# Feed-forward stage of a cross-attention block: sums of h and low parts moved from GpSimd to VectorE, squares moved to ScalarE, one set of weights kept over the change of batches, x1 + beta made beside x1

## The reference

```python
# attention block: 16 query heads, 4 key/value heads, head size 96, keys from 512 + 64 rows
x1 = x + attention(layernorm(x), ctx, Wq, Wk, Wv) @ Wo.T
# feed-forward block
z = layernorm(x1)
h = relu(z @ up_w) ** 2                       # 1024 -> 2048
r = sum(top_k(z @ gate_w, 2))                 # one factor per row
moe = ((z @ fc1_w) @ expert_w) * r            # 1024 -> 512 -> 512
y = h @ down_w + moe @ fc2_w                  # -> 1024
out = x1 + layernorm(y) * gamma + beta
```

## Time and profile before

| | us |
|---|---|
| median of 3 runs | 2124.26 (2122.04 to 2125.34) |
| the profiled execution | 2126.14 |
| its span | 2124.4 |
| PE busy | 1998.0 (94%) |
| DVE busy | 1251.8 (59%) |
| POOL busy | 1083.4 (51%) |
| ACT busy | 747.1 (35%) |
| output projection, tiles 0 to 15 | up to about 1216 |
| first product of the feed-forward | 1216 to 1692 |
| second product, norm and store | 1692 to 2124 |

### The profile page before, as it was taken

The page is one execution under the profiler, slowest core; times in us unless marked ns, Lnnn a source line. Parts: engine busy times, 40 slices in busy tenths (PEclk is TensorE's granted clock), DMA queues, the critical chain, the costliest instruction groups (busy, mean ns, idle before and its releaser), DMA issues.

```text
span 2124.4 us, 28447 instructions
## 1 busy us (share of the span) xinstructions
PE 1998.0 (94%) x9068; PEld 1656.9 (78%) x9068; DVE 1251.8 (59%) x1611; ACT 747.1 (35%) x1194; POOL 1083.4 (51%) x686
## 2 busy tenths in 40 slices
PE   8999999999999999999999779987799979999796
PEld 7888888888888888888887566866578768888685
DVE  4231312278888888812233479879778743456979
ACT  5021211167777777722110322123222233332131
POOL 2533030157777777652122156655765755456565
PEclk9999999999999999999999889988899989999998
DMA  6743433635566555345677665574343576765653
GB/s 198 263 152 138 168 119 100 174 96 147 151 157 157 149 147 146 102 150 180 188 250 229 232 178 198 195 231 169 119 149 139 176 243 198 242 198 170 218 184 136
DMA packets 352829, 368.32 MB, mean 173 GB/s; under 512 B 148704, under 2 KB 247008, under 8 KB 350304
## 3 DMA queue, kind: packets, MB, share of 16 engines
q1 hardware_dynamic: 284416, 303.56, 44.8%
q10 hardware_dynamic: 68320, 63.58, 11.0%
HBM read 241.99 MB, written 124.80 MB: 173 GB/s over the span
## 4 chain that ended last, share of the span: by engine, by line
PE 74%; DVE 10%; DMA 5%; issue 4%; POOL 3%; SPq 2%; ACT 1%; ACTq 1%; DVEq 0%; POOLq 0%
PE psum L139 22%; PE psum L140 22%; PE psum L141 22%; PE psum L1009 3%; POOL staging L2223 2%; DVE operands L1841 2%; DMA operands<-h_operand_scratch 2%; SPq L1355 1%; DMA operands<-o_scratch 1%; DMA z_turned_scratch<-plain 1%; ACTq L1355 1%; DVE plain L2523 1%; PE psum L1056 1%; PE psum L1036 1%; PE psum L1055 1%
## 5 line engine op out<-in xcount | busy, mean ns | idle before, releaser
L139 PE MATMUL psum<-operands 128*128 128x512 f32 (+3 forms) x2728 | 1062.2, 389 | 105.0 <-POOL operands L2370 24.4
L140 PE MATMUL psum<-operands 128*128 128x512 f32 (+3 forms) x2728 | 1058.3, 388 | 0.0
L141 PE MATMUL psum<-operands 128*128 128x512 f32 (+3 forms) x2728 | 1054.6, 387 | 0.0
L139 PEld LDWEIGHTS psum<-operands 128*128 128x128 f32 (+1 forms) x2728 | 519.3, 190 | 206.9 <-issue 34.9
L141 PEld LDWEIGHTS psum<-operands 128*128 128x128 f32 (+1 forms) x2728 | 519.6, 190 | 102.3
L140 PEld LDWEIGHTS psum<-operands 128*128 128x128 f32 (+1 forms) x2728 | 520.0, 191 | 89.9
L2370 POOL TENSOR_TENSOR operands<-operands 128x640 fp32r<-128x640 f32 x112 | 201.9, 1812 | 173.1 <-ACT operands L2366 172.8
L1183 DVE TENSOR_REDUCE small<-psum 128x1 fp32r<-128x576 f32 x256 | 192.8, 753 | 90.0 <-PE psum L1009 89.9
L2223 POOL TENSOR_TENSOR staging<-staging 128x1024 f32<-128x1024 f32 x50 | 149.2, 2986 | 145.8 <-DVE staging L2096 98.5
L926 POOL TENSOR_TENSOR operands<-staging,operands 128x512 fp32r<-128x512 f32 x128 | 164.5, 1293 | 30.3 <-ACT operands L1103 21.5
L1510 POOL TENSOR_TENSOR operands<-operands 128x384 fp32r<-128x384 f32 x64 | 66.4, 1053 | 209.8 <-ACT operands L1505 209.8
(11 more groups left out here) (148 smaller groups left out, 1912.4 us busy)
## 6 DMA issues: line engine op xcount, KB each, us to landing
h_operand_scratch<-staging SPq DMA_DIRECT2D x70, 512.0 KB, 2.9
operands<-h_operand_scratch SPq DMA_DIRECT2D x112, 320.0 KB, 4.0
plain<-in_up_w SPq DMA_DIRECT2D x32, 512.0 KB, 4.6
plain<-in_down_w SPq DMA_DIRECT2D x29, 512.0 KB, 5.8
operands<-recip_scratch SPq DMA_DIRECT2D x64, 192.0 KB, 3.9
o_scratch<-staging SPq DMA_DIRECT2D x64, 192.0 KB, 4.8
operands<-o_scratch SPq DMA_DIRECT2D x64, 192.0 KB, 3.3
operands<-q_hi_scratch ACTq DMA_DIRECT2D x14, 768.0 KB, 5.8
```

The lines of the kernel that those rows point to most:

```text
L139: e.matmul(o, lh, rh, start=first, stop=False)
L140: e.matmul(o, lh, rl, start=False, stop=False)
L141: return e.matmul(o, ll, rh, start=False, stop=last)
```

## The change

The diff touches the three stages above. In the output projection POOL adds beta to each tile of x1 behind the low parts of the next tile (`xb_add` in `c_pool`), and SP stores the sum between the store of x1 and the next load of x:

```diff
+        def xb_add(e, n):
+            e.wait_ge(*past(bet_l, 16 if n < XB_MOVES else 32))
+            e.wait_ge(*past(cc_x1, n + 1))
+            e.wait_ge(*past(cc_xs, 16 * n))
+            beta_row, to = xb_tiles(n)
+            e.tensor_tensor(to, XR, beta_row, ALU.add).then_inc(cc_xb, 1)
+
+        def xb_store(e, n):
+            e.wait_ge(*past(cc_xb, n + 1))
+            e.dma_start(xb_d[n * P:(n + 1) * P, :], xb_tiles(n)[1]).then_inc(cc_xs, 16)
...
                     e.dma_start(x1_d[bass.ds(n * P - P, P), :], XR).then_inc(cc_st, 16)
                     e.wait_ge(*past(cc_st, n * 16))
                     e.sem_inc(idle, 1)
+                    xb_store(e, n - 1)
                     c_load_x(e, n)
...
-                    if n == LAST_C - 2:
-                        d_first_loads(e)
+                    d_first_loads(e, n)
```

In the first product a set of weights `g` is loaded only in the iterations ahead of a new one (`prepare`); iterations 4 and 5, on both sides of the change of batches, share one:

```diff
+        CHUNKS = [0, 1, 3, 4, 2, 2, 0, 1, 3, 4]
+        GATED = [it for it in range(NIT) if CHUNKS[it] >= 3]
+        FIRST_STEP = [it for it in range(NIT) if it == 0 or CHUNKS[it] != CHUNKS[it - 1]]
...
-        W_SUMS, W_HI, W_LO_V, W_LO_G = [5, 6, 7, 3], [1, 5, 6, 2, 7, 3, 4], [5, 1, 6], [7, 2, 3, 4]
+        W_SUMS, W_HI = [5, 6, 7, 3], [1, 5, 6, 2, 7, 3, 4]
+        W_LO_V, W_LO_G = ([5, 1, 6], [5, 1, 6, 2, 7]), ([7, 2, 3, 4], [3, 4])
...
+            def square(it, part, h):
+
+                n = squares(it, part)
+                e.wait_ge(*summed(it, "c" + part))
+                e.activation(h, h, ACT.Relu).then_inc(d_rl, 1)
+                e.wait_ge(*past(d_rl, n))
+                e.activation(h, h, ACT.Square).then_inc(d_sq, 1)
...
                 e.wait_ge(*after_product(it, 1))
+                if it == 0:
+                    e.wait_ge(*past(cc_xb, B * ST))
...
+                if it == 0:
+                    e.wait_ge(*past(cc_xs, 16 * B * ST))
+                    e.wait_ge(*past(cc_st, 16 * B * ST))
                 e.tensor_tensor(O22, product_bank(it, 6), O11, ALU.add).then_inc(d_sm, 1)
-
-            def u5_sums(it):
                 e.wait_ge(*summed(it, "u"))
-                e.wait_ge(*past(d_s5, it + 1))
-                e.tensor_tensor(O12, O22, O12, ALU.add).then_inc(d_sm, 1)
+                e.wait_ge(*past(d_os[2], 16 * it))
+                e.tensor_tensor(O12, product_bank(it, 5), O22, ALU.add).then_inc(d_sm, 1)
```

In the second product SP loads x1 + beta, the POOL addition L2593 is gone, and the norms are spread:

```diff
+        def norm_after(g):
+
+            n = g - PASSES.index(6) * NPR
+            if n < 0:
+                return None
+            if n < 2 * NPR:
+                return n // 2 if n % 2 == 0 else None
+            return n - NPR
...
-                if PASSES[s] == 6 and pr >= 1:
-                    e_x1_load(e, pr - 1 + NX)
...
+                if norm_after(g - 2) is not None and norm_after(g - 2) + NX < NT_E:
+                    e_x1_load(e, norm_after(g - 2) + NX)
```

More of the change, by code:

```diff
@@ L1665, in xattn_ffn_kernel, with scaled, squares @@
         Z_SUMS, Z_HI, Z_LO_V, Z_LO_G = [5, 6, 7, 4], [1, 6, 5, 7, 2, 3, 4], [1, 5, 6, 7, 3], [2, 4]
-        W_SUMS, W_HI, W_LO_V, W_LO_G = [5, 6, 7, 3], [1, 5, 6, 2, 7, 3, 4], [5, 1, 6], [7, 2, 3, 4]
+        W_SUMS, W_HI = [5, 6, 7, 3], [1, 5, 6, 2, 7, 3, 4]
+        W_LO_V, W_LO_G = ([5, 1, 6], [5, 1, 6, 2, 7]), ([7, 2, 3, 4], [3, 4])
         SUM = {"u": 1, "u+p5": 2, "c11": 3, "u+p7": 4, "c22": 5, "c12": 6, "c21": 7}
-        READY = {"11": 1, "22": 2, "12": 3, "21": 4}
         def summed(it, what):
             return past(d_sm, 7 * it + SUM[what])
+        def scaled(it):
+            return it in GATED
+        def squares(it, part):
+            order = ("11", "12") if scaled(it) else ("11", "22", "12", "21")
+            return sum(2 if scaled(i) else 4 for i in range(it)) + order.index(part) + 1
         def h_ready(it, part):
-            return past(d_f, 4 * it + READY[part])
+            if scaled(it) and part in ("22", "21"):
+                return past(d_wt, 2 * GATED.index(it) + (1 if part == "22" else 2))
+            return past(d_sq, squares(it, part))
         def slot_bank(n):
@@ L2016, in d_act @@
             for it in range(NIT):
-                q, dc = it // NF5, it % NF5
-                nxt = it + 1 < NIT
+                q, g = it // NF5, weights_of(it)
+                prepare, end = it + 1 in FIRST_STEP, it == NIT - 1
+                if it and not scaled(it - 1):
+                    square(it - 1, "21", O21)
                 if it == NF5:
-                    z_hi(e, 1, 2)
                     z_hi(e, 1, 3)
                 e.wait_ge(*after_product(it, 1))
+                if it == 0:
+                    e.wait_ge(*past(cc_xb, B * ST))
                 e.wait_ge(*past(d_os[0], 16 * it))
@@ L2065, in d_act @@
                     z_hi(e, 1, 7)
-                if nxt:
-                    w_hi_op(e, it + 1, 3)
+                    z_hi(e, 1, 2)
+                if end:
+                    for n in range(3, NU):
+                        e_unit_hi(e, n)
+                square(it, "12", O12)
+                if prepare:
+                    w_hi_op(e, g + 1, 3)
+            assert scaled(NIT - 1)
         def d_dve(e):
@@ L2103, in weighted @@
                     m = e.tensor_tensor(half, half, RW_T[r], ALU.mult)
-                m.then_inc(d_f, 1)
-            def h21(it):
-                e.wait_ge(*after_product(it, 4))
-                e.tensor_tensor(O21, product_bank(it, 4), O21, ALU.add).then_inc(d_sm, 1)
-                e.wait_ge(*summed(it, "c21"))
-                if scaled(it):
-                    weighted(it, O21, 0)
-                else:
-                    squared(O21)
+                m.then_inc(d_wt, 1)
             def u_sums(it):
@@ L2150, in h12, with h21 @@
[L2150 to L2158 removed]
+            def h21(it):
+                e.wait_ge(*after_product(it, 4))
+                e.wait_ge(*summed(it, "u+p7"))
+                e.tensor_tensor(O21, product_bank(it, 4), O21, ALU.add).then_inc(d_sm, 1)
+                if scaled(it):
+                    e.wait_ge(*summed(it, "c21"))
+                    weighted(it, O21, 0)
@@ new lines, in add, with add_1, add_2_3 @@
+            def add(it, n, to, a, b, op):
+                if n in (3, 5):
+                    e.wait_ge(*past(d_hs, 5 * it + n - 1))
+                else:
+                    e.wait_ge(*past(d_os[{1: 4, 2: 5, 4: 6}[n]], 16 * it))
+                e.tensor_tensor(to, a, b, op).then_inc(d_hs, 1)
+            def add_1(it):
+                e.wait_ge(*h_ready(it, "11"))
+                e.wait_ge(*h_ready(it, "22"))
+                add(it, 1, OM1, O11, O22, ALU.add)
+            def add_2_3(it):
+                e.wait_ge(*h_ready(it, "12"))
+                add(it, 2, OM2, O12, O22, ALU.add)
+                add(it, 3, O12, O12, O11, ALU.subtract)
```

386 lines of the change are left out of this document (186 added, 200 removed).

## The result

The changed kernel takes 2112.21 us (median of 6 runs, 2107.76 to 2117.24) against 2124.61 for the kernel before (6 runs beside it): a ratio of 0.9947, 95% interval 0.9933 to 0.9962. It is faster by 0.5%, where 3.2% was forecast (2056 us, range 2034 to 2088). The sign was right; 56 us of the 68 did not come.

What follows compares the result with a forecast made beforehand. PE was taken as the bound, busy 94% of the span, so only its waits or the tail could pay. The terms -9 -3 +1.5 +5 -28 -2 -14 -14 -6 gave -69.5 us: 2056 us, range 2034 to 2088.

Steps and rivals of the forecast that it cites:

- Output projection: Output projection: POOL's added additions cost 0, the stall ahead of tile 14 goes; net -9 us, bounds -12 and +1.
- about 6 us of slack: Ordinary output projection tiles: this slack before the next unit is needed covers the 3 us by which SP's loads come later.
- SP held in the output projection: Rival, output projection: stores wait for POOL, each of 15 tiles loses 5 us, 2131 us in all; chance 0.05.
- Iteration 0: Start of the first product: the 18.2 us weights wait goes, but POOL's and SP's lateness takes nearly all; -3 us.
- Iterations 1 to 3: First product: later z_norm and loads cost +1.5 us in iterations 1 and 2, and +5 ahead of iteration 4.
- Iterations 4 and 5: First product: kept weights and fewer sums remove most stalls, 88 us instead of 116.2; -28 us, bounds -20 and -32.
- z low 7: Iteration 5: operand ready at about 67 us, wanted at 62 to 65; 2 to 5 of the 13.4 us stall stay.
- Iterations 6 to 9: First product: the one 1.9 us stall falls, DVE's and ACT's work stays hidden by PE; -2 us.
- Second product: Second product: -14 us from the third step's wait and -14 us from passes 6 and 5.
- the -14 of passes 6 and 5: Second product: half as many norms per step, so all three stalls fall, 11.0 us plus slow clock, less 2.
- Tail: Behind the last matmul: additions of beta fall, DVE is 3 us late instead of 9; -6 us, bounds 0 and -9.
- the signs that the prediction named: Wrong if PE idles ahead of every tile or DVE ends over 8 us late; right if iteration 5's stalls are under 5.

Runs made afterwards that it cites:

- experiment 3: Changed kernel with GpSimd's addition of x1 + beta placed ahead of the low part of the next tile's last unit, not behind it: 2103.1 us.
- no_xb: Changed kernel without x1 + beta in the output projection; GpSimd adds beta to x1 in the second product, as before the change: 2079.48 us.
- (5): Changed kernel with only the last tile's addition of x1 + beta moved to DVE, the fifteen others staying on GpSimd: 2105.4 us.
- xb_on_dve: Changed kernel with all additions of x1 + beta on DVE, right behind each tile's own addition, instead of on GpSimd: 2094.49 us.
- half_xb_norms: As half_xb, but with the second product's first eight normalizations all in pass 6 again: 2086.3 us.
- dve_xb_unstored: As xb_on_dve, but the sum x1 + beta is not stored and beta is left out of the output: 2088.18 us.
- (8): Changed kernel with iteration 5 loading and preparing its weights again, instead of keeping those of iteration 4: 2123.25 us.
- norms_old: Changed kernel with the second product's first eight normalizations all in pass 6 again, one a tile, and none in pass 5: 2102.46 us.
- 9: As no_xb, with iteration 3's transposition of the last z blocks on DVE moved behind the sums and the next first weights' low part: 2075.64 us.
- 13: As xb_on_dve, with z block transfers in pieces of 8 over tiles 7, 8, 11, 12 and transpositions one tile later: 2084.23 us.
- half_xb: Changed kernel with x1 + beta on DVE in the output projection for batches 0 and 2, beta on POOL for the other eight tiles: 2070.46 us.

## Why the prediction was wrong, point by point

**Output projection: the step that failed.** It said that the addition ends 3 us behind POOL's last low part, that SP's next loads come so much later, and that "about 6 us of slack" cover this: "Cost 0". Measured +32.7 in place of -9. The rest of the term was nearly right: without x1 + beta PE ended the stage at 1209.0, 7.4 us earlier than before. The addition was sized well, 2.45 us on average for the first 15, against 3.0. What was wrong is the wait that it was put behind. I timed it by one ordinary tile, whose low parts end 4 us in. In the changed kernel a tile's low parts run late wherever ACT was held: at tile 4 by a wait of 12.48 us for the expert weights, at tiles 7 and 11 by z transfers that took 10.1 and 8.7 us to issue. The addition, and with it x and the next units, waits for the low part of the last unit, so that SP's second store came 8.3, 12.1 and 14.9 us behind the first there. By the order of the code a late unit makes the next addition late in turn, so the slack, which I had counted afresh for every tile, is not there again; that taking the addition out from behind the last unit moved the stage end by 15 us (3) agrees with this. The rival "SP held in the output projection" named this place, at a chance of 0.05, but asked for a delay of 10.6 us everywhere; the stage ends 40 us later than in no_xb, a mean loss of 2.7 us over 15 tiles.

How it divides, by the medians: 9 us by the order on POOL (experiment 3), 7 by the place of the last addition (5), 18 for both and for POOL's own time (4). xb_on_dve is still 15 over no_xb. At the stage's end that is 23.5 us, because no_xb pays some 16 later in the second product and the tail. Of the 23.5, 3.1 are there by tile 10, 3.7 come over tiles 11 and 12, and 16.7 over tiles 13 to 15, where DVE's addition of tile 13 stands behind z's third norm, as in half_xb_norms (11). What makes xb_on_dve and dve_xb_unstored 3 to 4.5 us late by tile 10 in the first place is not settled; it is not the second store (6). Nor is it shown by a run what turns tiles 13 to 15 slow.

**Iteration 0** (-3, measured -0.9). The waits stood as forecast: POOL's first operation starved (13.19 us, forecast 10), SP's z work behind it (L1377 at 1268.52, 19 us behind the last tile; forecast 17), a stall at product 2 (9.11; forecast 10), iteration 1 61.8 us behind the last tile (62 to 66). The stall at product 2 is only in part the added operation's, though: in no_xb a low part is POOL's first operation at this place and took 10.46 us, and PE waits 6.79 us there. The delay of SP's z work is its doing: in no_xb iteration 1 starts 53 us behind the last tile.

**Iterations 1 to 3** (+6.5, measured +13.5). Iteration 4 starts 55 us behind iteration 3 (forecast 53): right. Iterations 1 and 2 are the mis-sized term, +6.7 and not +1.5: gate_out was waited for 6.47 and 2.39 us. In no_xb it was 2.32 and 2.34, so 4 of these 5 us are x1 + beta again; the three iterations take 143.7 us there, 8.4 over before.

**Iterations 4 and 5** (-28, measured -23.7). The first two stalls went as said. z low 7 kept 7.42 us, not 2 to 5, and with its slow clock that is the difference. Keeping the weights is worth 11.0 (8).

**Iterations 6 to 9** (-2, measured -3.4). PE is busy for all 158.30 us. ACT's squares, a Relu and a Square on 128x1024, cost 1.06 us an operation and hid. The changes of set, an estimated 13 us by the Trainium skill (ScalarE: Activation LUTs, section on table sets), did not come: the trace has four table loads, as many as before.

**Second product** (-28, measured -27.5). The sum was right and one reason was not: the third step kept 3.7 of 12.6, where 1.5 was forecast, but the -14 of passes 6 and 5 came from POOL's additions leaving; the spread norms that I credited gave nothing (7).

**Tail** (-6, measured +0.3). "DVE 3 us late at the end instead of 9" failed: it is 9.6 us late, and in norms_old, with the eight norms in pass 6, not late at all. I put DVE's 60 us of work in pass 5's 54.6 down as covered. The work was sized right, 59.45 us busy, but DVE took 66.5 us for it, from its first sum of pass 5 (1995.78) to its first of pass 7 (2062.27), 12 us behind PE. In pass 7 it takes 5.3 to 8.3 us a tile against PE's 6.8, so most of that backlog came out at the end.

Of the signs that the prediction named, three spoke against it: PE idle ahead of tiles (not every one, but seven of the sixteen by over 2 us), DVE more than 8 us behind PE at the end, and a stall of over 5 us left in iteration 5.

So: of 60.5 us missed, some 48 hang on x1 + beta (42, 2 and 4), 6 on the norms' place, 4 on z low 7, and 2 on iteration 3. That the second product's sum came out although one of its reasons was wrong was luck.

## What to carry to other kernels

A wait put into the queue that loads the next inputs must be costed by the latest thing it stands behind in the worst tiles, not by its own duration in an ordinary one; slack is spent once and not afresh in every tile, because lateness in a load comes back as lateness of the next wait. Work that is moved to where engines are idle is cheap only if the loads do not wait for it: doing half of it, on the engine that had just made its input, took 2070.5 us, against 2094.5 for all of it there and 2079.5 for none (with the moves of 7, 9 and 13 as well, all of it came to 2071.3). And when operations are spread to thin out one stretch, look at what the next stretch already holds, for most of a backlog in front of the last pass is paid behind the last matmul.

## What the runs showed of the hardware

An addition of 128x1024 on POOL took 13.19 us while DVE ran six operations in a row on SBUF operands, from 1253.30 to 1264.46, each at its uncontended length (1.22 and 2.29). It ended at 1266.71, 2.25 us after them, which is about what it takes alone (2.45 on average of the 15 others): it got next to no turn while they ran. The prediction had an operation of 10.33 us at this place, and in no_xb it is 10.46. It isn't the rule: beside the addition at 1213.16 (3.25 us on POOL) DVE was the one stretched, 4.48 us for a sum of 128x2048 that takes 2.29 elsewhere. Which of the two yields is not worked out. The Trainium skill (VectorE: DVE Perf Modes, section on two Vector instructions with no wait between them) has the shared interface; the price seen here is 10.7 us for one operation. DVE operations on one column with two SBUF tensors were stretched as well: 657 ns on average without POOL's additions in the second product (the changed kernel), 1076 with them (no_xb), 0.16 us at the end of pass 7; the one-column operation with a single tensor (L2590 and L2577) took 154 and 153 ns.
```profile
L2591 DVE TENSOR_TENSOR small<-small 128x1 f32<-128x1 f32 x16 | 10.5, 657 | 0.6
```
```profile
L2578 DVE TENSOR_TENSOR small<-small 128x1 f32<-128x1 f32 x16 | 17.2, 1076 | 0.6
```
One program can take quite different courses through the output projection: half_xb and half_xb_norms have the same instructions up to there and end the stage at 1216.7 and 1232.7. Single runs of one kernel fall 9 to 15 us apart; whether by the same cause is not shown, since only one run of each has a trace. Sixteen transfers of 64 KB in a row took ACT 8.7 to 13.4 us to issue; what sets the length within that was not tested.
